# Attention in tiles: the last group of two tiles becomes two groups of one tile, whose steps take two blocks of keys

## The reference

```python
# feed-forward stage, twice (layers l = 0, 1)
x = x + attn(ln(x)) ;  h = ln(x) ;  x = x + moe(h)     # l = 0: experts by token, l = 1: by sequence
# attn, for each head
att = q @ k.T * hd ** -0.5
att = where(causal, att, -inf)                          # not in the mixing stage
y = softmax(att) @ v
```

## Time and profile before

| | us |
|---|---|
| median of three runs | 3146.79 (3143.51 to 3146.86) |
| the profiled execution | 3150.18 |
| its span, first to last instruction | 3148.5 |
| busy: PE, DVE, ACT, POOL | 2659.7 (84%), 2638.5 (84%), 2248.2 (71%), 588.9 (19%) |

### The profile page before, as it was taken

One profiled execution on the slowest core, in us unless ns is written; L12 is line 12 of the kernel. 1 busy time (PEld: TensorE's weight loads), 2 busy tenths in 40 slices (PEclk: granted clock), 3 DMA queues, 4 the chain that ended last, 5 costly groups with the idle time before them and its releaser, 6 DMA issues. The chain is left out here.

```text
span 3148.5 us, 71461 instructions
## 1 busy us (share of the span) xinstructions
PE 2659.7 (84%) x28144; PEld 1162.4 (37%) x28144; DVE 2638.5 (84%) x3552; ACT 2248.2 (71%) x4330; POOL 588.9 (19%) x1125
## 2 busy tenths in 40 slices
PE   3469999899799995759999999579998998899976
PEld 3332333577423333412222222222333776323325
DVE  5758899788798995769999999389998887899976
ACT  1137888676578884439999999458988676689864
POOL 3123100344321001100000000032101543321011
PEclk8668999999899997969999999789999998899998
DMA  1061000215310000230000000150000314300001
GB/s 33 1 149 41 23 14 14 59 45 108 73 31 21 14 12 25 67 70 9 13 12 14 12 12 12 49 114 25 16 16 15 74 51 98 73 22 18 15 12 31
DMA packets 109883, 119.09 MB, mean 38 GB/s; under 512 B 20726, under 2 KB 87660, under 8 KB 109548
## 3 DMA queue, kind: packets, MB, share of 16 engines
q1 hardware_dynamic: 102444, 98.21, 12.3%
q0 software_dynamic: 4608, 13.96, 2.4%
q10 hardware_dynamic: 2496, 2.36, 0.4%
HBM read 70.31 MB, written 43.78 MB: 36 GB/s over the span
## 5 line engine op out<-in xcount | busy, mean ns | idle before, releaser
L1480 ACT ACTIVATE h_probsf<-h_ps_lowf 128x512 f32<-128x512 f32 (+3 forms) x812 | 424.3, 551 | 131.3 <-PE h_ps_lowf L1414 80.2
L1480 ACT ACTIVATE h_probsg<-h_ps_lowg 128x512 f32<-128x512 f32 (+3 forms) x812 | 424.3, 551 | 118.2 <-PE h_ps_lowg L1414 76.5
L1480 ACT ACTIVATE h_probsb<-h_ps_lowb 128x512 f32<-128x512 f32 x683 | 389.1, 596 | 79.4 <-PE h_ps_lowb L1414 61.2
L1435 PE MATMUL h_ps_valuesf<-h_probsf,v_all 128*9 128x256 f32 (+2 forms) x4608 | 354.2, 380 | 40.3 <-POOL h_probsf L1578 33.1
L1435 PE MATMUL h_ps_valuesg<-h_probsg,v_all 128*9 128x256 f32 (+2 forms) x4608 | 350.2, 376 | 30.2 <-POOL h_probsg L1578 22.8
L1435 PE MATMUL h_ps_valuesb<-h_probsb,v_all 128*9 128x256 f32 x4096 | 318.4, 383 | 9.3 <-ACT h_drainedb L1489 5.0
L1528 DVE TENSOR_REDUCE h_maxima_0b<-h_ps_scanb 128x2 f32<-128x1024 f32 x256 | 292.4, 1213 | 29.9 <-PE h_ps_scanb L1376 29.9
L1528 DVE TENSOR_REDUCE h_maxima_2b<-h_ps_scanb 128x2 f32<-128x1024 f32 x256 | 292.7, 1214 | 6.7 <-PE h_ps_scanb L1376 6.7
L1528 DVE TENSOR_REDUCE h_maxima_0f<-h_ps_scanf 128x2 f32<-128x1024 f32 x224 | 259.1, 1216 | 21.8 <-PE h_ps_scanf L1376 21.2
L1528 DVE TENSOR_REDUCE h_maxima_0g<-h_ps_scang 128x2 f32<-128x1024 f32 x224 | 258.7, 1215 | 19.3 <-PE h_ps_scang L1376 18.6
L1480 ACT ACTIVATE h_probsf<-h_ps_highf 128x512 f32<-128x512 f32 (+3 forms) x404 | 224.1, 555 | 38.0 <-PE h_ps_lowf L1414 35.2
(11 more groups left out here) (483 smaller groups left out, 5230.5 us busy)
## 6 DMA issues: line engine op xcount, KB each, us to landing
q_stack<-combine_weights SPq DMA_DIRECT2D x64, 256.0 KB, 3.6
q_stack<-in_L_ffn_e_w SPq DMA_DIRECT2D x24, 256.0 KB, 3.2
q_stack<-q_parts SPq DMA_DIRECT2D x22, 256.0 KB, 6.0
k_stack<-k_parts SPq DMA_DIRECT2D x22, 256.0 KB, 8.2
attended<-h_drainedf SPq DMA_DIRECT2D x16, 256.0 KB, 2.9
attended<-h_drainedf SPq DMA_DIRECT2D x32, 128.0 KB, 1.9
attended<-h_drainedb SPq DMA_DIRECT2D x32, 128.0 KB, 1.9
attended<-h_drainedg SPq DMA_DIRECT2D x16, 256.0 KB, 2.2
```

What stands on the lines that cost most here:

```text
L1435: last = nc.tensor.matmul(ps_values[32 * j:32 * j + VD, low:high], m.v_all[:, kb, QUAD * quad + j, :], probs[:, (u + j % banks) % RING_P, ...
L1480: nc.scalar.activation(by_head(probs[:, of % RING_P, :], of), by_head(ps_scores[of % RING_S], of), ACT.Exp, scale=SOFTMAX_SCALE).then_inc( ...
```

## The change

Only the last group of each attention changes. In its place stand two groups of one tile each: tile 2, then tile 3, of the same chunk and quad. A masked attention has 25 groups then, the unmasked 33. A step of a one-tile group takes two blocks of keys (`span`), so that a unit still has 512 columns: 2 blocks x 2 heads x 128 queries. Tile 2 (masked) has 15 blocks and 8 steps, the last with one block; tile 3 has 16 blocks and 8 steps. Units are 32, as before.

- Scores of a full step: 8 products of 128 columns instead of 4 of 256. Values: 8 products (4 heads, 2 blocks) of 128 columns instead of 4 of 256.
- Search: the same pieces, in the order tile 2 (6 full, 2 diagonal), tile 3 (6 full, 2 diagonal); one more row maximum, turn, negation and shift (four more small DMAs), one more drain and write, each drain of half the width.
- Selects: two for tile 2 (its last step) and two for tile 3 (its last step), four in all, as before. `inverse_deviation` stands ahead of the first select of the *last* group, so now behind the two of tile 2.
- Two more tensors for the maxima in each attention, and two more memsets ahead of it.
- Plan works out PE's order anew from the same costs.

```diff
+CAUSAL_ORDER[-1:] = FULL_ORDER[-1:] = [(CHUNKS - 1, 1)] * 2
...
-        self.steps = [(g, kb) for g in range(len(self.groups)) for kb in range(self.blocks[g])]
+        self.steps = [(g, kb) for g in range(len(self.groups)) for kb in range(0, self.blocks[g], self.span(g))]
...
-        return ((0, 2), (3,)) if n == TPC else ((0, 1),) if t0 == 0 else ((2,), (3,))
+        return ((t0,),) if n == 1 else ((0, 2), (3,)) if n == TPC else ((0, 1),) if t0 == 0 else ((2,), (3,))
...
-        return QUAD * self.groups[g][3] // TPC
+        return max(2, QUAD * self.groups[g][3] // TPC)
+
+    def span(self, g):
+        return 2 if self.groups[g][3] == 1 else 1
+
+    def keys(self, g, kb):
+        return range(kb, min(kb + self.span(g), self.blocks[g]))
+
+    def hides(self, g, kb):
+        c, _, t0, _ = self.groups[g]
+        return self.causal and self.keys(g, kb)[-1] >= TPC * c + t0
...
-        return QUAD // self.banks(g) * (self.queries(g) - self.offsets[self.step_of[u]])
+        g, kb, _ = self.units[u]
+        return len(self.keys(g, kb)) * (QUAD // self.banks(g)) * (self.queries(g) - self.offsets[self.step_of[u]])
...
-                free = now + 2 * (ROWS_NEXT + 2 * COLUMN * (high - low))
+                free = now + 2 * self.span(self.steps[n][0]) * (ROWS_NEXT + 2 * COLUMN * (high - low))
...
-                at = kb % TPC * P
-                for i in range(QUAD // plan.banks(g)):
-                    pair = 2 * quad + k // 2 + i
+                for i, (block, head) in enumerate((block, head) for block in plan.keys(g, kb) for head in range(per)):
+                    pair, at = 2 * quad + k // 2 + head, block % TPC * P
...
-                for j in range(QUAD):
+                for i, block in enumerate(plan.keys(g, kb)):
+                    for j in range(QUAD):
...
-                at = by_head(probs[:, u % RING_P, :], u)[:, :, 0:P]
+                heads = QUAD // plan.banks(units[u][0])
+                at = by_head(probs[:, u % RING_P, :], u)[:, -heads:, 0:P]
```

27 lines of the change are left out of this document (14 added, 13 removed).

## The result

The changed kernel is slower: median 3160.63 us of five runs (3155.47 to 3162.46) beside 3146.86 of the kernel before in the same session (five runs, 3143.51 to 3149.61). The ratio is 1.0037, 95% interval 1.0024 to 1.0050, about 12 us. The profiled execution took 3162.46, its span is 3160.7, against 3150.18 and 3148.5 before.

The account below looks back on a forecast made before the run. No engine was full on average; at attention ends, PE's `finish` products and POOL's selects held ACT back. Terms -2 x 0.6 + 2 x 0.9 + 0.8 = 1.4 us faster gave 3145.4 us, range 3125 to 3157.

Parts of the forecast that it names:

- Two units run at once, until 564.1: Attention 1: tile 2's first two units follow the group before, ending at 563.0, without a wait.
- now 565.6: Attention 1: end of POOL's four selects ahead of the drain, 565.31 before; drained at 566.5.
- Two of the `finish` products (1.03 each) now lie between them; I charge 1.5: Attention 1: delay by `finish` products among tile 2's remaining steps, 1.5 us, bounds 0 and 2.1.
- four steps behind the third `rows` product: Attention 1: four of tile 3's eight steps remain behind that product, so the last exponential ends at 588.6.
- The end of attention 1 (and 4): Terms there together made each 0.6 us slower; bounds 2.5 faster, and 1.7 slower with five steps, 2.8 with six.
- Attentions 2 and 5: Half of 2.9 us more idle time regained, 1.45 - 0.6: each 0.9 faster, bounds 1.7 slower and 5.4 faster.
- The step's cost: Two-block steps: 0.06 us more PE time each, score pairs every 0.07 us, nothing on the path.
- C: Rival: products of 128 columns go one at a time, 26 us over 80 steps, 3172; chance 0.03.
- 2.5 faster: Attention 1's bound on the fast side, if the `rows` products wait for nothing.
- A: Rival: ACT's gaps at the attentions' ends close, `finish` fitting PE's free time: 23.5 us faster, 3123; chance 0.25.
- B: Rival: POOL's order makes `inverse_deviation` late, five or more steps behind third `rows` product: 3154, six steps 3158.5; chance 0.22.
- D: Rival: Plan keeps tile 2's scores behind `finish`, only the second change of groups is left, 6 us: 3153; chance 0.05.

Follow-up runs that it names:

- e6: Changed kernel with tile 2's scores and first `finish` product ahead of the values waiting for selects, `rows` products left in place: 3151.80 us, ratio 1.0009.
- e4: Changed kernel with both edits, e2's and e3's: 3148.02 us, ratio 0.9990 to the kernel before.
- e1: Kernel before with only the unmasked attention's last group split into two one-tile groups: 3147.83 us, ratio 0.9995.
- e11: e4 with the second `finish` product moved behind the last waiting value piece and the third `rows` product one step later: 3141.36 us, ratio 0.9970.
- e17: e11 with DVE's bias far ahead, before the first scan maximum of the fourth group: 3138.20 us, ratio 0.9963.
- e2: Changed kernel with POOL's `inverse_deviation` ahead of tile 2's two selects: 3164.73 us, ratio 1.0048.
- e3: Changed kernel, planner reckoning 3.3 us for the selects ahead of tile 2, so its scores precede the waiting values in PE's list: 3166.39 us, ratio 1.0049.
- e16: Kernel before with only DVE's bias moved behind the scalings: 3159.49 us, ratio 1.0030.
- e13: Changed kernel with DVE's bias moved behind the three scalings: 3169.80 us, ratio 1.0065.

## Why the prediction was wrong

Taking the end of the group before (562.65 before, 559.09 after, 563.0 in the prediction) as zero in attention 1:

| | before | predicted | after |
|---|---|---|---|
| tile 2's first exponentials | | 0 | 3.8 |
| the group's drain ends | 6.9 | 3.5 | 5.2 |
| tile 2's last exponential ends | | 12.2 | 16.6 |
| `inverse_deviation` begins | 9.0 | 13.1 | 17.1 |
| normalising begins | 10.1 | 14.2 | 18.2 |
| third `rows` product | 15.7 | 19.8 | 24.1 |
| last exponential ends | 25.3 | 25.6 | 30.0 |

**"Two units run at once, until 564.1" is the step that failed first.** It took tile 2's scores as free to run once their shift was in. They were in PE's list behind a value piece that waits for the selects, which I had looked up in its old place only. It brought ACT 3.80 us of idle time where I had none. Not all of that was lost, as the drain behind them waits for the selects in any case: the drain ends 1.7 us behind the prediction.

**The selects' end, "now 565.6", failed with it.** I had them end 2.6 us behind the group's exponentials; they end 3.75 behind (562.84). In either kernel they end 4.9 us behind the last negation, as DVE's instructions set it and not their own start. The sum moved that negation by the 1.2 us of one more maximum and turn, and the selects by only 0.3. This is 1.1 of the 1.7 us. That they begin nearer to the bias now (0.25 us behind its start, 1.33 before) is why they last 4.72 instead of 3.63.

**The charge for the `finish` products is the largest term that failed: "Two of the `finish` products (1.03 each) now lie between them; I charge 1.5".** All three lie between tile 2's steps, and ACT idled 2.44 + 1.11 + 0.89 = 4.44 us for them, 2.9 more than charged. The third ran at the full clock and cost 0.89. The first two took 2.08 and 1.38 us instead of 1.16, as the clock was at its lower level behind PE's wait of 2.88; I had reckoned with 1.00 in attention 1.

So 1.7 us are lost up to the drain and 2.7 from there to tile 2's last exponential. From that row on every row of the table is 4.0 to 4.4 us behind the prediction, and nothing more is lost: selects ahead of `inverse_deviation`, 1.07 to `normalise`, four steps behind the third `rows` product, 1.08 a step. These steps held.

- **The end of attention 1 (and 4):** tails 4.6 and 4.9 us longer, 0.6 predicted. In attention 1, e6 takes back 2.3 of it and e4 1.9 more.
- **Attentions 2 and 5:** 2.3 and 2.4 longer, 0.9 shorter predicted. The idle time there was the same kind, and the low clock didn't shrink: over the whole tail its mean fell from 0.92 to 0.89. 1186 to 1191 has 0.50, 1203 to 1207 has 0.58, where the earlier trace rows had 0.60.

```profile
1187.24 1.08 ACT L1498 ACTIVATE h_probsf<-h_ps_lowf 128x512 f32<-128x512 f32 x2 [3.68 <-PE h_ps_lowf L1431]
```
```profile
1186.00:1191.00 5.00, 4.85 (x52) 3.04 (x48) 1.48 (x3) 2.39 (x5) 1.30 (x2) 0.50 0.08 26
...
1203.00:1207.00 4.00, 3.98 (x48) 2.55 (x48) 3.68 (x8) 1.09 (x2) 0.74 (x1) 0.58 0.01 3
```

- **Attention 3:** 1.0 shorter, 0.8 predicted; e1 shows it alone. There is nothing to wait for, and its gaps between `finish` products are 0.89 instead of the earlier trace rows's 3.60.
- **The step's cost** held. The first and last of eight score products in a row, attention 1 after:

```profile
572.52 0.23 PE L1431 MATMUL h_ps_lowf<-q_stack,k_stack 49*128 49x128 bf16 x1
...
572.71 0.22 PE L1431 MATMUL h_ps_highf<-q_stack,k_stack 49*128 49x128 bf16 x1
```

Eight start within 0.19 us, a pair every 0.06, where C needed 0.14; e4 says the same in time. By the Trainium skill's sustained 81 ns for each product of 128 columns ("TensorE: Matmul & The Clock Gate", Back-to-back issue gap) they would start within 0.57 us, as an estimate; the trace differs, and decides. The eight are pairs in two row halves of the array, and no run here has a longer row of them.

- **A bound:** "2.5 faster" doesn't follow from the terms named with it, which give 2.9 - 1.5 - 0.95 - 0.3 + 2.8 = 2.95. Nothing that was measured rests on it.

**The rivals.** A (the gaps close) is not even reached by the tuned lists: e11 and e17 are 9 and 12 us faster than the kernel before, not 23.5. B came nearest in time (3154, with six steps 3158.5). Its condition, a late `normalise`, was met, but its mechanism wasn't: four steps stood behind the third product, not five or more, and `inverse_deviation` first by itself changed nothing (e2). C is refuted by the spacing of the scores and by e4. D had the right subject, Plan's order, but not this order: tile 2's scores were ahead of `finish` and behind the values. The errors, 4.0 and 4.3 in attentions 1 and 4, 3.2 and 3.3 in 2 and 5 and -0.2 in 3, make 14.7 (before rounding); added to 3145.4 they give 3160.1, where 3160.63 was measured. That it comes so near is partly luck: by the ratio the change cost 11.7 us, by the tails 13.3.

## What to carry to other kernels

Where an order of instructions is fixed ahead, an item is priced by what stands in front of it in the list, not by when its input is ready; print the new list before pricing any part of it. Where several such lists wait for each other, one edit to one list (e2, e3) can bring nothing where two together (e4) bring 15 us, so a change that loses should be tried again with the lists that it disturbed adjusted. And a planner's cost for an operation (here the same for every select) has to be the one of its place: 0.41 us alone, 4.7 for four beside DVE's two-operand instructions. Waits of PE have a second price that the wait itself doesn't show, the lower clock behind them, and two attentions with the same lists can differ by 1.2 to 1.4 us in it.

## What the hardware showed that I had not expected

- POOL's select of 0.41 us lasted 1.21 (before), 2.29 (after), 3.02 (e16) and 4.09 (e13), each time until 0.27 us behind the end of an instruction or an unbroken run of instructions with two operands on DVE. Moving DVE's bias of 2.27 us behind the scalings cost the kernel before 9 us (e16): PE waits 3.16 us for the selects instead of 1.80, and the clock falls behind it in attentions 1 and 4 too.
- PE's clock: it fell to the lower level during or within 1.3 us behind all four waits of 2.88 us in the changed kernel. The length of one wait doesn't settle it. Behind 1.80 us in attention 1 before, 1.00 was granted for the 4.3 us that follow; behind the same 1.80 us in attention 2 before, it was 0.60 over 1184 to 1188:

```profile
1182.79 0.62 PE L1435 MATMUL h_ps_valuesf<-h_probsf,v_all 128*9 128x256 f32 x8 [1.80 <-POOL h_probsf L1578]
```

Three short waits (0.57, 0.67, 0.67) were followed by the lower level in all four masked attentions of e3 and in two of the four of e4.
